# Attention with condition, one core of a Trainium2: softmax denominators from sums of four key tiles, and a fourth bank for maxima products

## The reference

```
x = x + attention(rmsnorm(x, cond))          # softmax over 1024 keys, 16 heads of 32
x = x + swiglu(rmsnorm(x, cond))             # hidden width 2048
out = x_in + x
attention: p = softmax(q @ k.T / sqrt(32)); o = p @ v; out = o @ Wo.T
```

## Time and profile before

| | us |
|---|---|
| runs of the kernel before (3) | 2542.66, 2549.76, 2553.31; median 2549.76 |
| profiled execution, its own time | 2545.35 |
| span of the profile | 2543.2 |
| TensorE busy in the span | 2382.3 (94%) |
| VectorE, ScalarE, GpSimd busy | 1710.1, 1310.6, 1108.1 |
| granted TensorE clock, mean | 0.984 of full |

### The profile page before, as it was taken

One profiled execution on the slowest core, in us unless ns is written; L12 is line 12 of the kernel. 1 busy time (PEld: TensorE's weight loads), 2 busy tenths in 40 slices (PEclk: granted clock), 3 DMA queues, 4 the chain that ended last, 5 costly groups with the idle time before them and its releaser, 6 DMA issues. The chain is left out here.

```text
span 2543.2 us, 39928 instructions
## 1 busy us (share of the span) xinstructions
PE 2382.3 (94%) x11396; PEld 1578.0 (62%) x11396; DVE 1710.1 (67%) x2732; ACT 1310.6 (52%) x2287; POOL 1108.1 (44%) x1063
## 2 busy tenths in 40 slices
PE   5999989999989999989999875999999999999999
PEld 4644436544437444447444344888888888888887
DVE  4766744666735766736667536887787778877877
ACT  3356662556662566653656734436344534453444
POOL 0255551355550555541555534650464147316611
PEclk8999999999999999999999997999999999999999
DMA  6212213212112222132122153115511542154125
GB/s 200 53 40 56 52 30 105 45 43 63 51 31 87 51 52 54 46 92 52 39 53 51 47 166 116 51 33 163 195 57 54 165 166 59 60 173 150 50 75 174
DMA packets 92655, 209.62 MB, mean 82 GB/s; under 512 B 15632, under 2 KB 15632, under 8 KB 90640
## 3 DMA queue, kind: packets, MB, share of 16 engines
q1 hardware_dynamic: 91344, 202.71, 27.2%
q0 software_dynamic: 1088, 4.19, 0.5%
HBM read 134.23 MB, written 19.92 MB: 61 GB/s over the span
## 5 line engine op out<-in xcount | busy, mean ns | idle before, releaser
L410 POOL TENSOR_TENSOR sums<-probs 128x512 f32<-128x512 f32 x512 | 653.3, 1301 | 791.7 <-ACT probs L558 789.2
L632 DVE TENSOR_REDUCE pmax<-bank 128x1 f32<-128x512 f32 x1024 | 654.7, 684 | 282.0 <-PE bank L842 271.0
L558 ACT ACTIVATE probs<-bank 128x512 f32<-128x512 f32 x1024 | 584.5, 597 | 398.7 <-PE bank L926 365.4
L926 PE MATMUL bank<-qs,ks 128*128 128x512 f32 x1024 | 458.0, 452 | 29.2 <-ACT probs L558 28.6
L842 PE MATMUL bank<-ks,qs 96*128 96x512 f32 x1024 | 403.3, 407 | 25.5 <-DVE pmax L632 25.4
L926 PEld LDWEIGHTS bank<-qs,ks 128*128 128x128 f32 x1024 | 191.0, 187 | 369.5 <-ACT probs L558 225.0
L1489 PE MATMUL bank<-H_hi,wt_hi 128*128 128x512 f32 x896 | 350.0, 391 | 14.8 <-DVE H_lo L1344 14.6
L1503 PE MATMUL bank<-ow,aw 128*128 128x512 f32 x1536 | 358.6, 392 | 0.0
L1489 PE MATMUL bank<-H_lo,wt_hi 128*128 128x512 f32 x896 | 349.3, 390 | 0.0
L1489 PE MATMUL bank<-H_hi,wt_lo 128*128 128x512 f32 x896 | 349.3, 390 | 0.0
L1503 PEld LDWEIGHTS bank<-ow,aw 128*128 128x128 f32 x1536 | 285.6, 188 | 59.8 <-issue 1.2
(11 more groups left out here) (135 smaller groups left out, 3138.3 us busy)
## 6 DMA issues: line engine op xcount, KB each, us to landing
raw<-in_gu_w SPq DMA_DIRECT2D x66, 512.0 KB, 3.6
wo_raw<-in_out_w SPq DMA_DIRECT2D x128, 256.0 KB, 2.8
ks<-qk_hi SPq DMA_DIRECT2D x136, 128.0 KB, 2.4
qs<-qk_hi SPq DMA_DIRECT2D x264, 64.0 KB, 2.0
x<-in_x SPq DMA_DIRECT2D x10, 1024.0 KB, 5.7
ks<-qk_lo SPq DMA_DIRECT2D x68, 128.0 KB, 2.4
qs<-qk_lo SPq DMA_DIRECT2D x132, 64.0 KB, 2.0
wv<-wv_parts SPq DMA_DIRECT2D x4, 2048.0 KB, 8.7
```

Source lines behind the costliest of these rows:

```text
L410: nc.gpsimd.tensor_tensor(sums[:, h, :], probs[:, 0, h, :], probs[:, 1, h, :], ALU.add) \
L558: nc.scalar.activation(probs[:, s % 2, h, :], sbank[i % SB][:], ACT.Exp, scale=SCALE).then_inc(st_done, 1)
L632: nc.vector.reduce_max(pmax[:, t, h, hf:hf + 1], mbank[n % MB][:], AX_X).then_inc(sq_done, 1)
L926: nc.tensor.matmul(sbank[i % SB][:], ks[:, g % 2, h, s * P:(s + 1) * P], qs[:, u % 3, h, :], start=True, stop=True).then_inc(st_ready, 1)
```

## The change

It does four things. (1) GpSimd adds four key tiles instead of two before a denominator product: at s % 4 = 1 it adds two tiles of `probs`, at s % 4 = 2 and 3 it adds one more tile to `sums`. That makes 24 adds in a unit instead of 16. (2) A unit then has two denominator tiles D instead of four accumulated pairs. They go through the work bank: D 0 at (5, 2), D 1 at (1, 2) of the next unit (`SUMS_AT`). ScalarE copies D 0 to `den`; VectorE adds D 1 to it from the bank. The first add of the next four key tiles waits until the D product before is done (`w_ready`), since `sums` is single. (3) `dbank` is gone and the maxima products get a fourth bank, MB = 4. (4) The slots of projections and hT tiles move to make room in the work bank, and behind the last unit the order of VectorE and TensorE changes: VectorE takes the first output tile before the denominators, and the last D product stands behind the second output product instead of the first.

```diff
-PAIRS = 4
+QUADS = 2
+QT = 4
 for odd in (1, 3):
-    PROJECTED.update({("Q", odd + 2): (odd * UNIT, 2), ("K", odd + 3, 0): (odd * UNIT + 18, 2),
+    PROJECTED.update({("Q", odd + 2): (odd * UNIT + 8, 2), ("K", odd + 3, 0): (odd * UNIT + 16, 1),
                       ("K", odd + 3, 1): ((odd + 1) * UNIT, 1), ("Q", odd + 3): ((odd + 1) * UNIT + 9, 2)})
-PROJECTED.update({("Q", NU - 1): (5 * UNIT, 2), ("Q", NU): (6 * UNIT, 2), ("K", NU, 0): (7 * UNIT + 16, 2),
+PROJECTED.update({("Q", NU - 1): (5 * UNIT + 8, 1), ("Q", NU): (6 * UNIT + 8, 2), ("K", NU, 0): (7 * UNIT + 15, 1),
                   ("K", NU, 1): (7 * UNIT + 24, 2)})
-HT_AT = {5: (10, 14, 18, 22), 7: (0, 4, 8, 12)}
+HT_AT = {5: (13, 16, 19, 24), 7: (0, 3, 9, 12)}
+SUMS_AT = {(5, 2): (0, 0), (1, 2): (1, 1)}
-SB, MB = 2, 3
+SB, MB = 2, 4
...
-    obank, dbank, wbank = psum[5], psum[6], psum[7]
+    obank, wbank = psum[6], psum[7]
...
@@ GpSimd
-                        for h in range(GH if s % 2 else 0):
+                        for h in range(GH if s % QT else 0):
                             pool.wait_ge(st_done, SCORES_T(b, NT + n * GH + h + 1) + SB)
-                            if h == 0:
-                                pool.wait_ge(d_ready, products_done(b, u, s // 2))
-                            nc.gpsimd.tensor_tensor(sums[:, h, :], probs[:, 0, h, :], probs[:, 1, h, :], ALU.add) \
+                            if s % QT == 1 and h == 0:
+                                pool.wait_ge(w_ready, MISC(b, sums_before(u, s // QT)))
+                            if s % QT > 1:
+                                pool.wait_ge(sum_done, sums_done(b, u, s - 1, h))
+                            first = probs[:, 0, h, :] if s % QT == 1 else sums[:, h, :]
+                            nc.gpsimd.tensor_tensor(sums[:, h, :], first, probs[:, s % 2, h, :], ALU.add) \
                                 .then_inc(sum_done, 1)
@@ ScalarE, work_tile
+                elif tile[0] == "D":
+                    u = tile[1]
+                    act.wait_ge(on_done, b * NU + (u + 1))
+                    nc.scalar.activation(den[:], bank[:], ACT.Copy).then_inc(w_act, 1)
@@ ScalarE, exponentials
-                            if s % 2 == 0:
-                                act.wait_ge(sum_done, sums_done(b, u, s // 2 - 1, h) if s
-                                            else sums_done(b, u - 1, PAIRS - 1, h))
+                            if s % QT != QT - 1:
+                                act.wait_ge(sum_done, sums_done(b, u, s - 2, h) if s >= 2
+                                            else sums_done(b, u - 1, NS + s - 2, h))
@@ VectorE, work_tile
+                elif tile[0] == "D":
+                    nc.vector.tensor_tensor(den[:], bank[:], den[:], ALU.add).then_inc(w_dve, 1)
@@ VectorE, behind the last unit
-                for t in range(3):
+                for t in range(2):
                     lo_part(t)
+                out_tile(0)
+                for t in range(2, 4):
+                    lo_part(t)
+                work_tile(b, ("D", NU - 1, 1))
                 for part in range(4):
                     normalise(b, NU - 1, part)
@@ TensorE
-            def denominators(b, u, pair):
-                pe.wait_ge(sum_done, sums_done(b, u, pair, GH - 1))
-                if pair == 0:
-                    pe.wait_ge(od_act, b * (2 * NU) + (2 * u + 2))
+            def denominators(b, u, quad):
+                work_bank_empty(b, ("D", u, quad))
+                pe.wait_ge(sum_done, sums_done(b, u, QT * quad + QT - 1, GH - 1))
                 for h in range(GH):
-                    last = nc.tensor.matmul(dbank[DH * h:DH * h + DH, :], ones[:], sums[:, h, :], start=(pair == 0),
-                                            stop=(pair == PAIRS - 1))
-                last.then_inc(d_ready, 1)
+                    last = nc.tensor.matmul(wbank[DH * h:DH * h + DH, :], ones[:], sums[:, h, :], start=True, stop=True)
+                last.then_inc(w_ready, 1)
...
-                                if s % 2 == 0:
-                                    denominators(b, u if s else u - 1, (s // 2 - 1) % PAIRS)
+                            if sums_at(u, s, h):
+                                denominators(b, *sums_at(u, s, h)[1:])
```

More of the change, by code:

```diff
@@ L89, in misc_order @@
     return list(IN_V.values()) + [tile for u in range(NU) for s in range(NS) for h in range(GH)
-                                    for tile in done_at(u, s, h)]
+                                    for tile in done_at(u, s, h)] + [("D", NU - 1, 1)]
 def part_at(u, s, h):
@@ L105, in made_at, with sums_at @@
     return ("mT", u + 1) if (s, h) == MAXIMA_AT and u < NU - 1 else None
+def sums_at(u, s, h):
+    back, quad = SUMS_AT.get((s, h), (NU, 0))
+    return ("D", u - back, quad) if u >= back else None
 def next_maxima(u, s, h):
@@ L116, in done_at, with act_reads, dve_reads @@
     tile, part = part_at(u, s, h) or (None, 0)
-    return [m for m in (made_at(u, s, h), tile if part == KT - 1 else None) if m]
+    return [m for m in (made_at(u, s, h), tile if part == KT - 1 else None, sums_at(u, s, h)) if m]
+def act_reads(tile):
+    return (tile[0], tile[-1]) != ("D", 1)
+def dve_reads(tile):
+    return tile[0] != "mT" and (tile[0], tile[-1]) != ("D", 0)
 LEAD_MISC = misc_order(False)
@@ L122 @@
 MISC = Counter(len(LEAD_MISC), len(BODY_MISC))
-LEAD_DVE = [m for m in LEAD_MISC if m[0] != "mT"]
-BODY_DVE = [m for m in BODY_MISC if m[0] != "mT"]
+MISC_ACT = Counter(sum(map(act_reads, LEAD_MISC)), sum(map(act_reads, BODY_MISC)))
+LEAD_DVE = [m for m in LEAD_MISC if dve_reads(m)]
+BODY_DVE = [m for m in BODY_MISC if dve_reads(m)]
 MISC_DVE = Counter(len(LEAD_DVE), len(BODY_DVE))
@@ L138, in misc_index, with sums_before @@
     return (BODY_MISC if body else LEAD_MISC).index(tile)
+def sums_before(u, quad):
+    if quad:
+        return misc_index(True, ("D", u, 0)) + 1
+    return misc_index(True, ("D", u - 1, 1)) + 1 if u else 0
 def slot_users(tile):
@@ L152, in qk_slot, with sums_done, act_before @@
     return tile[2] if tile[0] == "K" else 0
[L155 to L162, removed]
+def sums_done(b, u, s, h):
+    return b * (NU * SUMS) + (SUMS * (u + 1) + GH * (s // QT * (QT - 1) + max(s % QT, 1) - 1) + h + 1)
+def act_before(body, tile):
+    order = BODY_MISC if body else LEAD_MISC
+    return sum(map(act_reads, order[:order.index(tile)]))
 def dve_before(body, tile):
     order = BODY_MISC if body else LEAD_MISC
-    return sum(m[0] != "mT" for m in order[:order.index(tile)])
+    return sum(map(dve_reads, order[:order.index(tile)]))
 def hold(sp, held, semaphore, value):
@@ L274, in lead_bank @@
         def lead_bank(i):
-            return (wbank, obank, dbank, mbank[0])[i % LEAD_BANKS]
+            return (wbank, obank, mbank[1], mbank[0])[i % LEAD_BANKS]
         def x_tokens(b, hf):
@@ L366, in _ @@
                 hold(sp, held, pv_done, b * (NU * NS) + NU * NS + 2)
-                hold(sp, held, sum_done, sums_done(b, NU - 1, PAIRS - 1, GH - 1))
+                hold(sp, held, sum_done, sums_done(b, NU - 1, NS - 1, GH - 1))
                 load_wv()
@@ L564, in _ @@
                             for tile in done_at(u, s, h):
-                                work_tile(b, tile)
+                                if act_reads(tile):
+                                    work_tile(b, tile)
                             if (s, h) == (NS - 1, 0) and u < NU - 1:
@@ L614, in work_tile @@
                 dve.wait_ge(w_ready, MISC(b, misc_index(body, tile) + 1))
-                dve.wait_ge(w_act, MISC(b, misc_index(body, tile) + 1))
+                if act_reads(tile):
+                    dve.wait_ge(w_act, MISC_ACT(b, act_before(body, tile) + 1))
                 bank = wbank if body else lead_bank(misc_index(body, tile))
@@ L743, in _ @@
                             for tile in done_at(u, s, h):
-                                if tile[0] != "mT":
+                                if dve_reads(tile):
                                     work_tile(b, tile)
@@ L762, in out_tile @@
                     nc.vector.tensor_copy(yout[:, t % 2, :], mbank[n % MB][:]).then_inc(sq_done, 1)
-                for t in range(3):
+                for t in range(2):
                     lo_part(t)
+                out_tile(0)
+                for t in range(2, 4):
+                    lo_part(t)
+                work_tile(b, ("D", NU - 1, 1))
                 for part in range(4):
                     normalise(b, NU - 1, part)
-                for t in range(NT):
+                for t in range(1, NT):
                     out_tile(t)
@@ L794, in work_bank_empty @@
                 if b is not None:
-                    pe.wait_ge(w_act, MISC(b, i))
+                    pe.wait_ge(w_act, MISC_ACT(b, act_before(True, tile)))
                     pe.wait_ge(w_dve, MISC_DVE(b, dve_before(True, tile)))
```

30 lines of the change are left out of this document (11 added, 19 removed).

## The result

The changed kernel takes 2638.06 us (median of 4 runs, 2630.10 to 2651.71) against 2551.53 (2542.66 to 2556.98) for the kernel before (median of 4): ratio 1.0348, 95% interval 1.0295 to 1.0401. Forecast was 2490. The profiled execution took 2630.10, 84.8 more than the one of before; the sum had said 55 less. I name a stretch as the prediction does: a half unit runs from the score (1, 2) to (5, 2), or from (5, 2) to (1, 2) of the next unit.

What follows compares the result with a forecast made beforehand. TensorE was taken to set the pace in attention. The terms -62.1 - 20 + 26 - 11 + 5 + 4 - 5 + 8 = -55 took the profiled 2545.35 us to 2490, forecast 2478 to 2502, wider range 2462 to 2522.

Steps and rivals of the forecast that it cites:

- Added: eight adds per unit: 256 more adds on GpSimd, half idle; a round of 16.2 us fits a mean half unit, costing +4 us.
- the moved query and key parts: Query parts now in slots 8 to 15, each three matmuls, about 0.6 us and at most 0.85.
- The row of 1.64 us: Profile row for VectorE's multiply of `o` by `den`: 1.11 us on average, 1.64 at 588.21.
- the rule of the Trainium skill: Two-SBUF-input VectorE instructions and SBUF-reading GpSimd ones exclude each other; hT differences up to 1.64 us, 20 us, outside the sum.
- the stall at (2, 3): Behind the product at (1, 2), scores wait for GpSimd's adds, shortened by query parts: +5 us (0 to +12).
- Removed products: TensorE's denominator products drop from 32 to 16 per batch, 64 fewer at 0.97 us: -62.1 us.
- Fourth bank: A fourth maxima bank lets TensorE run one product further ahead of VectorE: -20 us (0 to -25.4).
- The stall behind D 0: GpSimd's adds start later behind the product at (5, 2); score (6, 3) waits 0.91 us: +26 (0 to +36).
- mT and hT: mT tile's wait covered by the new wait at (6, 3), -11 us; unit 5's closer hT tiles +8 (0 to +16).
- Small half units: Half units from an even to an odd unit, and unit 6 to 7, end at GpSimd's round of 16.2 us.
- The rivals: Four alternatives: about 2515 us (chance 0.16), 2470 (0.15), 2590 (0.08), and nothing gained, 2530 to 2555 (0.06).
- C: Slower rival: GpSimd bounds everywhere, adds over 1.46 us apart, at 1.50 about 2590 us; chance 0.08.

Runs made afterwards that it cites:

- e2: Changed kernel with GpSimd's adds at s % 4 = 2 made 8 columns wide, one key tile of four left out of the denominators: 2574.78 us, ratio 1.0088.
- e7: Changed kernel with odd units' query tile back in slots 0 to 3 and the adds at s % 4 = 2 eight columns wide: 2537.07 us, ratio 0.9939.
- e1: Changed kernel with the query tile of odd units projected in slots 0 to 3 instead of 8, 10, 12, 14: 2627.89 us, ratio 1.0306.
- e9: Changed kernel with the multiply of `o` by `den` replaced by a one-input transpose of `den`, wrong values: 2601.76 us, ratio 1.0185.
- e3: Kernel before with only odd units' query tile moved to slots 8, 10, 12, 14 and the first half key tile to 16 to 19: 2576.66 us, ratio 1.0108.
- e4: Kernel before with the denominator products of pairs 0 and 2 left out, adds and all else kept: 2501.90 us, ratio 0.9802.
- e6: Changed kernel with three maxima banks as before, the fourth left unused: 2671.61 us, ratio 1.0453.

## Why the prediction was wrong

Two steps failed, and both were left at or near nothing: "Added: eight adds per unit", whose price on VectorE was put beside the sum and not into it, and the moved query and key parts, which were counted as matmuls alone.

- **GpSimd's added load.** The prediction counted the adds for GpSimd's own round and found slack. That part held: the distance is 1.24 (5.04 us for four, 9.99 for eight), the product waited for `sums` 0.7 us in all. What failed is who else pays. The row of 1.64 us stood in the prediction, and the rule of the Trainium skill was priced at 20 us by taking 1.64, the longest multiply of before, as the longest hold, with only the hT differences as victims, and then not used. The runs show 63 us (e2), 91 once the other cause is gone (e7 against e1), and the multiply, not hT, as the largest part that was taken out by itself (e9: 36). The Trainium skill (SBUF — State Buffer, "Who interferes with whom") says that whichever comes first gets the shared access "for the whole instruction", and that `tensor_scalar` can take it too, in some of its modes. The trace agrees on who is held (the multiply with two inputs 2374 ns, the transpose with one 704 in e9; the scaling of `x` 475 before, 1277 now) and goes beyond it on for how long: 3.70 and 4.70 us, over several instructions, to the end of a run of adds.
- **Moved parts.** A step that moves takes its DMAs with it. The prediction moved three matmuls per part to slots 8 to 15 and asked only what they do for the stall at (2, 3). From the first of the twelve DMAs to the landing of the last go 8.9 us (536.23 to 545.11), and the key tile is complete 4.7 after that first (540.9), since only five slots lie between. Worth 27 us by itself (e3), about 10 taken out of the changed kernel alone (e1), and 38 taken out beside the lighter load (e7 against e2).
- **Removed products.** -62 forecast, -48 measured (e4). A product is worth 0.9 in place of 0.97, which makes some 4 of the 14; the rest shows as the seven half units at a lower clock.
- **Fourth bank.** -20 forecast, 33 measured (e6), in a kernel with longer VectorE stalls to bridge. Right mechanism, larger size. But the waits for `pmax` that should have gone only went from 25.4 to 21.3, since the held multiply brings new ones.
- **The stall behind D 0.** Forecast +26 with 0.91 at (6, 3). In unit 2 of the kernel after the release takes 0.12 (product's end 590.33, add 590.45; estimate 0.16), and TensorE waits 0.16, 0.49 and 0.68 for exponentials, at (6, 1), (6, 3) and (7, 2), 1.33 in all where 0.91 stood. Right in kind, half as large again. In e7, where little else holds these, waits for exponentials are 78.7 us against 28.6, so +50 where +26 and +5 stood.
- **mT and hT.** The -11 for mT came to -2: its wait fell from 11.1 to 4.7, but 4.6 came back at the same product as a wait for `hT_lo`. hT tiles cost TensorE 27.7 us of waits for VectorE against 8.4 before, so +19 where +8 was forecast; with the narrow adds (e2) they are at 11.6, so most of it goes with GpSimd's load.
- **Small half units.** 16.2 forecast, 17.1 measured, e.g. 587.70 to 604.80. GpSimd's twelve adds take 14.86 there as computed, but the next product comes at its place in TensorE's order 1.05 behind them.
- **The rivals.** None was right. C's figure (2590) lies nearest, by a mechanism that hardly occurred: the adds are 1.25 apart in units 1 and 2 and up to 1.40 where they take turns with scalings or hT differences, and the product doesn't wait for them. What should have stood as the slower rival is "VectorE is held for whole runs of adds".
- **Clock.** The prediction took 1.00 for granted because before had it. Most stalls of 1.5 us and more were followed by a stretch at half clock, some were not (e1). What the clock costs in all was not taken apart from the waits; one kind of half unit at 0.92 and 1.00 differs by 1.5 us.

The sum, put right as an estimate: e7 has both causes mostly out (its multiply is at 1035 ns) and stands at 2537, 47 above the forecast. 14 of these are the products' shortfall and, if all of it counts, 19 the larger wait for exponentials; the rest, 14, stays open. The other 101 are the two causes together.

That a hold lasts until the run of adds ends is read from ends that coincide, in 15 multiplies, in 20 of e1, and from the 8-column ones. What decides whether a multiply gets in between two adds (618.37) or not (582.42) was not tried and stays open.

## What to carry to other kernels

Work moved to an idle engine can be paid for by an engine that shares its memory access. Here the price depended on how long GpSimd ran without a rest, and on whether TensorE had to wait for what stood behind the held instruction. Before adding, list the other engine's instructions that fall into the new unbroken run, and move them into the rest first. When a table moves a step, follow its buffer and its DMAs to the next user of that buffer, with the issue distance of the queue. And price two new stalls together: removing one alone (e1) showed 10 us of what was worth 38 once the other was gone too.

## What the chip showed beyond this

- A VectorE instruction with two SBUF inputs that starts inside GpSimd's back-to-back adds mostly either gets in behind the add in progress (0.94 us) or ends 0.55 us behind the last of the run, up to 4.70 us after its start (5.43 in e1). Its size adds no more than its own work (8 columns: up to 3.5 us), and a one-input transpose of 128x512 passes at 704 ns.
- Single waits of 1.5 to 1.8 us in otherwise busy stretches were followed by a granted clock of 0.50 (1.2 GHz) in nine of twelve cases (e1, units 1 to 3). Work there takes nearly twice as long: 1.94 us for a product of 1.07, behind the wait of 2.41 us in the kernel after.
